# Selective scan in one core: a sequence's statistics in one slot, its normalising over three, one subtraction by halves

## The reference

```
xz = hidden_states @ in_proj_w.T
x, z = jnp.split(xz, 2, axis=-1)
...                                    # causal convolution of 4 taps, silu
delta = jax.nn.softplus(delta + dt_proj_b.reshape(N_HEADS, H_DIN))
def step(s, inp):
    d_t, u_t, B_t, C_t = inp
    dA = jnp.exp(d_t[..., None] * A)
    s = s * dA + (d_t * u_t)[..., None] * B_t[:, :, None, :]
    y_t = jnp.einsum('bhdn,bhn->bhd', s, C_t)
    return (s, y_t)
...
y = y + x * Dskip
y = y * jax.nn.silu(z)
```

## Time and profile before

| | us |
|---|---|
| median of three runs | 3590.76 |
| the profiled execution's own time | 3593.5 |
| its span, first to last instruction | 3591.7 |
| selective scan, first slots without a scan | 1880 to 1976.9 |
| selective scan, first to last scan step's end | 1976.9 to about 3014 |
| mixture and store after it | 3014 to 3591.7 |

### The profile page before, as it was taken

How to read it: one execution, slowest core, us unless ns; L and a number is a source line. 1 busy time by engine, 2 the same in 40 slices (tenths; PEclk the granted TensorE clock), 3 DMA queues, 4 the chain that set the end, 5 groups by cost and what they waited for, 6 DMA issues and landing times. The chain is left out here.

```text
span 3591.7 us, 45021 instructions
## 1 busy us (share of the span) xinstructions
PE 2679.7 (75%) x12336; PEld 1880.9 (52%) x12336; DVE 2211.8 (62%) x3886; ACT 1544.3 (43%) x2662; POOL 2124.8 (59%) x1697
## 2 busy tenths in 40 slices
PE   4699995997579998449983767867867866599900
PEld 4599982443468897429981322322322323389900
DVE  4766553675566564673320989989989887733312
ACT  4333334663433333423334556546646633433300
POOL 0477761322057776335544988988888685355467
PEclk9899996777589999559996889999999998599955
DMA  6011112000401111602232877878877876122222
GB/s 170 18 47 47 46 40 58 24 24 1 124 28 47 45 47 32 188 9 70 70 71 63 277 264 267 278 255 273 286 243 267 280 251 195 31 64 71 69 69 76
DMA packets 286348, 429.39 MB, mean 120 GB/s; under 512 B 58332, under 2 KB 195839, under 8 KB 286240
## 3 DMA queue, kind: packets, MB, share of 16 engines
q1 hardware_dynamic: 250784, 357.34, 30.2%
q0 software_dynamic: 35456, 70.86, 8.3%
HBM read 367.51 MB, written 62.39 MB: 120 GB/s over the span
## 5 line engine op out<-in xcount | busy, mean ns | idle before, releaser
L600 POOL DMA_INDIRECT m_rows<-rows_in,m_source x568 | 552.0, 972 | 361.8 <-PE m_T_ps L628 211.5
L1497 PE MATMUL s_y_ps<-s_prod,ident 128*128 128x512 f32 x1024 | 549.0, 664 | 281.1 <-DVE s_prod L1766 281.0
L1759 DVE TENSOR_TENSOR_SCAN s_dA<-s_dA,s_dBu 128x1024 f32<-128x1024 f32 x256 | 586.2, 2290 | 146.4 <-POOL s_dBu L1457 72.3
L1457 POOL TENSOR_TENSOR s_dBu<-s_du,s_B_row 128x1024 f32<-128x1024 f32 x256 | 602.8, 2358 | 104.5 <-DVE s_dA L1759 97.0
L634 PE MATMUL m_A_ps<-m_rowsT,m_own 128*128 128x256 f32 x2272 | 566.5, 382 | 2.0 <-ACT m_rowsT L681 1.1
L650 PE MATMUL m_Y_ps<-m_own,m_hid 128*128 128x128 f32 x4544 | 554.3, 275 | 3.6 <-issue 3.6
L650 PEld LDWEIGHTS m_Y_ps<-m_own,m_hid 128*128 128x128 f32 x4544 | 529.8, 192 | 5.7 <-issue 5.6
L1497 PEld LDWEIGHTS s_y_ps<-s_prod,ident 128*128 128x128 f32 x1024 | 192.0, 205 | 600.4 <-DVE s_prod L1766 404.7
L634 PEld LDWEIGHTS m_A_ps<-m_rowsT,m_own 128*128 128x128 f32 x2272 | 412.9, 192 | 48.3 <-ACT m_rowsT L681 1.9
L1587 ACT ACTIVATE s_dA<-s_delta,s_decay 128x1024 f32<-128x1024 f32 x256 | 285.6, 1118 | 336.3 <-DVE s_prod L1766 329.7
L691 ACT ACTIVATE m_act_a<-m_A_ps,m_own 128x256 f32<-128x256 f32 x568 | 238.5, 471 | 433.8 <-PE m_A_ps L634 302.5
(11 more groups left out here) (229 smaller groups left out, 3789.0 us busy)
## 6 DMA issues: line engine op xcount, KB each, us to landing
s_B_row<-s_bc_rows SPq DMA_DIRECT2D x256, 512.0 KB, 5.6
s_C_row<-s_bc_rows SPq DMA_DIRECT2D x256, 512.0 KB, 5.7
rows_out<-m_y_sb SPq DMA_DIRECT2D x142, 128.0 KB, 1.9
rows_in<-m_xs SPq DMA_DIRECT2D x64, 256.0 KB, 3.2
m_rows<-rows_in,m_source POOLq DMA_INDIRECT x568, 2.5
s_got<-rows_by_token SPq DMA_DIRECT2D x16, 512.0 KB, 5.1
m_got<-rows_by_token SPq DMA_DIRECT2D x32, 256.0 KB, 4.2
rows_by_token<-m_y_sb,m_target POOLq DMA_INDIRECT x284, 2.3
```

The lines of the kernel that those rows point to most:

```text
L600: pool.indirect_dma_start(rows[:, b % 2, r, :], None, c.rows_in, bass.IndirectOffsetOnAxis(source[:, 2 * b + r:2 * b + r + 1], 0)).then_in ...
L1457: nc.gpsimd.tensor_tensor(dBu[q % RING][:, :], du[s % 2][:, h, :], B_row[q % RING][:, :], ALU.mult).then_inc(dBu_ready, 1)
L1497: ins = nc.tensor.matmul(y_ps[:, at(cc, 512)], c.ident[:, :], prod[q % 2][:, at(cc, 512)], start=(n == 0), stop=(n == NS - 1))
L1759: nc.vector.tensor_tensor_scan(dA[q % 2][:, :], dA[q % 2][:, :], dBu[q % RING][:, :], 0.0, ALU.mult, ALU.add).then_inc(scanned, 1)
```

## The change

DVE: `scales(t)` moves from slot 6 to slot 5, right behind `statistics(t)`. POOL: `take_root(t)` moves from slot 7 to slot 6. ACT: the eight tiles of `normalise` are spread over slots 7 (four), 8 (two) and 9 (two). ACT: e1 - 1 becomes two operations over one half each, the first in slot 26 and the second in slot 27, behind the dA made in slot 27; POOL's subtraction of half h waits only for half h. The counts of the semaphore `soft_act` go from 6 to 7 in a sequence.

```diff
             def soften(t, h, i):
                 done = t * 4 * HALVES + 4 * h
                 if i == 0:
-                    pool.wait_ge(soft_act, t * 6 + 6)
+                    pool.wait_ge(soft_act, t * 7 + 6 + h)
...
-                if t is not None and i == 7:
+                if t is not None and i == 6:
                     take_root(t)
...
-            def normalise(t):
-                act.wait_ge(norm_step, t * 2 + 2)
-                if t > 0:
-                    Use("turned", t - 1, 1).read(act)
-                for j in range(TILES):
+            def normalise(t, tiles):
+                if 0 in tiles:
+                    act.wait_ge(norm_step, t * 2 + 2)
+                    if t > 0:
+                        Use("turned", t - 1, 1).read(act)
+                for j in tiles:
...
                 nc.scalar.activation(du[t % 2][:, :, :], e1[:, :, :], ACT.Ln).then_inc(soft_act, 1)
-                act.wait_ge(soft_act, t * 6 + 5)
                 for k in (2, 3):
                     Use("dt", t, k).taken(act)
-                nc.scalar.activation(e1[:, :, :], e1[:, :, :], ACT.Identity, bias=minus_one[:, :]).then_inc(soft_act, 1)
+
+            def rounded_part(t, h):
+                act.wait_ge(soft_act, t * 7 + 5)
+                nc.scalar.activation(e1[:, h, :], e1[:, h, :], ACT.Identity, bias=minus_one[:, :]).then_inc(soft_act, 1)
...
-                    if i == 9:
-                        normalise(t)
+                    if 7 <= i < 10:
+                        normalise(t, (range(4), range(4, 6), range(6, 8))[i - 7])
...
                     if i == 26:
                         logarithm(t)
+                    if 26 <= i < 28:
+                        rounded_part(t, i - 26)
...
                     if i == 5:
                         statistics(t)
-                    if i == 6:
                         scales(t)
```

More of the change, by code:

```diff
@@ L1658, in exponent @@
                 nc.scalar.activation(e[:, h, :], e[:, h, :], ACT.Exp, scale=-1.0).then_inc(soft_act, 1)
-                act.wait_ge(soft_act, t * 6 + h * 2 + 1)
+                act.wait_ge(soft_act, t * 7 + h * 2 + 1)
                 nc.scalar.activation(e1[:, h, :], e[:, h, :], ACT.Identity, bias=1.0).then_inc(soft_act, 1)
             def logarithm(t):
-                act.wait_ge(soft_act, t * 6 + 4)
+                act.wait_ge(soft_act, t * 7 + 4)
                 wait(act, dBu_ready, (t - 1) * ALLN)
                 nc.scalar.activation(du[t % 2][:, :, :], e1[:, :, :], ACT.Ln).then_inc(soft_act, 1)
-                act.wait_ge(soft_act, t * 6 + 5)
                 for k in (2, 3):
                     Use("dt", t, k).taken(act)
-                nc.scalar.activation(e1[:, :, :], e1[:, :, :], ACT.Identity, bias=minus_one[:, :]).then_inc(soft_act, 1)
+            def rounded_part(t, h):
+                act.wait_ge(soft_act, t * 7 + 5)
+                nc.scalar.activation(e1[:, h, :], e1[:, h, :], ACT.Identity, bias=minus_one[:, :]).then_inc(soft_act, 1)
             def step(q):
```

## The result

The changed kernel takes 3586.43 us (median of 12 runs, 3580.28 to 3590.37), the kernel before, run beside it, 3593.64 us (12 runs, 3589.01 to 3600.63). The ratio is 0.998, with a 95% interval of 0.9971 to 0.9989: 7.2 us faster, between 4.0 and 10.4.

A forecast was written before the change was run, and what follows sets the result against it. DVE sets the time, so only its waits count. Terms 6.2 + 2.2 + 0.2 - 0.2 + 1.6 = 10.0 us (unrounded 9.9) take 3590.8 to 3580.9 us; 8-in-10 range 3575 to 3587.5.

The forecast's parts named there:

- rival (c): Slot 28: the split gives nothing because POOL's chain or a row of B comes last there; 3587.1 us, chance 0.10.
- slot 28, seven windows: Half the subtraction leaves ACT's chain before scan 28, 0.88 us in each of seven windows, 6.2 us gained.
- slots 10 and 11, sequences 1 to 7: Fewer tiles ahead of ACT's z copies let scan 11 start earlier in sequences 2, 3 and 6; 2.2 us gained.
- slots 10 and 11, sequence 0: In sequence 0 about 0.2 us is free in slot 11.
- statistics, slots 5 and 6: Dependent aggregates lose 0.7 us, the small variance operation goes from 4.0 to 3.5 us over seven windows; 0.2 us lost together.
- first window: Before the first scan: the root starts 0.7 us earlier and the half subtraction saves 0.88; 1.6 us gained.
- 2.00 - 1.12 = 0.88: Slot 28: whole subtraction 2.00 us less a half taken as 1.12, so ACT's chain gets 0.88 us shorter.
- what is late next: After slot 28: POOL's chain moves by the same 0.88 us, so scan 32 isn't left behind; B_row could be.
- rival (e): POOL late in slot 6: a held gather costs from 2.1 us of hold on, 2.3 us once; seven times 3610.2, chance 0.02.
- one hold in 96 gathers speaks against it: The argument against a held gather in all seven windows: only one, of 5.54 us in sequence 5, was seen.
- The shared port: DVE's small variance operation waits for POOL's whole running product; in sequence 6 it goes from 1.29 to 2.15 us.

The follow-up runs named there:

- e_order: The changed kernel with the wait for Ln ahead of the two bank waits again, only the first half waiting; one run, 3740.39 us against 3753.92 before.
- e_split: The kernel before with only the subtraction halved; 3722.71 us against 3733.49 before, ratio 0.9971.
- e_move: The kernel before with all of the change but the halved subtraction; 3729.64 us, ratio 0.9991 to the kernel before.
- before_again: The kernel before, unchanged, run once more on another chip; one run, 3749.68 us.
- e_add7: The changed kernel with the second add_out in slot 7 instead of slot 9; 3710.69 us against 3753.92 before, ratio 0.9884.
- e_pool: The changed kernel with the two small operations on 8 columns made by POOL ahead of the root, instead of DVE; one run, 3740.33 us.
- e_root7: The changed kernel with the root back in slot 7 and the tiles in slots 8 (six) and 9 (two); one run, 3720.52 us.

## Why the prediction held, and where its sum was off

The sign and the size held, and the time lies inside the range: 3586.43, predicted 3580.9. Of the 5.5 us between them, 2.9 are the kernel before, whose 12 runs have a median of 3593.64 where the three had 3590.76. The other 2.7 are the gain: 7.2 us (4.0 to 10.4) where the sum said 9.9. The interval holds both figures, so the runs alone don't show that the sum was off, nor do they tell the forecast from rival (c), whose 3587.1 lies nearer; that takes the slots. There the two pairs of profiles put the stage's gain at 6.04 us where the terms for the stage add up to 8.4. The sum beside them:

| term | predicted | two profiles before to two after |
|---|---|---|
| slot 28, seven windows | -6.2 | -5.43 |
| slots 10 and 11, sequences 1 to 7 | -2.2 | -3.28 |
| slots 10 and 11, sequence 0 | -0.2 | -1.05 |
| statistics, slots 5 and 6 | +0.2 | +0.58 |
| slot 17 | none | +1.19 |
| held gather, sequence 5 slot 9 | none | +2.10 |
| first window | -1.6 | -2.5 |

Only slot 28 is the same in both pairs, and the statistics nearly so (0.45 and 0.71). The other rows are means of unlike values: slots 10 and 11 gained 3.9 and 2.7 us, in sequence 0 0.2 and 1.9, the hold cost 1.5 and 2.7, slot 17 1.0 and 1.4, the first window gained 1.7 and 3.4. It is luck, too, that slots 10 and 11 gave 1.9 us more than the sum had and so covered more than half of what slots 17 and 9 took.

**The split: right, mis-sized.** The term "2.00 - 1.12 = 0.88" measured 0.78. Half the subtraction takes 1.15 us and not 1.12, the nearest row I had taken (dA), and the rewritten order of waits costs 0.08, as e_order shows. Nothing came late behind it: rival (c) falls, with the step into slot 28 at 6.12 in all seven windows and slots 29 to 32 as before.

**The spread: right, a little small.** That ACT's tiles hold slot 11, and PE's z once they are gone, is shown by e_split against e_move. I counted 0.95 us at most for a window, with gains in three; the step into slot 11 gains 0.5 to 0.9 in sequences 1 to 5 and loses 0.3 in 6; in the second pair it gains 0.4 to 0.9 and loses 0.4. In sequence 7, which normalises nothing, it is 0.5 and 0.3 shorter as well. The working took the end of z in each sequence from the one trace of before as fixed, and it isn't: in before_again, the same kernel, it ends 2.20 us after scan 10 in sequence 1 and 2.52 in sequence 4, where the first trace had 3.75 and 3.65. In the changed kernel it is 2.90 or 2.91 in five of seven. That the granted clock decides this, by when PE is back at its upper level (2.4 GHz) in slot 9, fits the rows of PE in sequence 3, where the sum takes 3.07 us and the z behind it 1.89, but was not tried by itself. In the changed kernel the granted clock of 2398 to 2406 was 0.64, and PE was busy 3.32 us of those 8:

```profile
2398.00:2406.00 8.00, 3.32 (x5) 1.51 (x5) 4.76 (x4) 1.62 (x3) 7.64 (x5) 0.64 0.96 299
2412.00:2430.00 18.00, 18.00 (x44) 7.93 (x44) 17.83 (x11) 9.82 (x11) 16.23 (x10) 1.00 0.85 271
```

**Slot 17: a give-back that was missing.** The step that failed is the one on slot 11, "what is late next": I asked it of slot 28 and not here. The second row above shows PE busy 18.00 of 18 us in slots 12 to 16; before, the same slots (2415 to 2433) had 17.78. DVE's finish of the sum then waits 0.22 us for it, and the step into slot 17 is 4.84 instead of 4.50:

```profile
2431.02 1.28 DVE L1757 SCALAR_TENSOR_TENSOR s_y<-s_u,s_d_skip,s_y_ps 128x1024 f32<-128x1024 f32 x1 [0.22 <-PE s_y_ps L1497]
```

It is so in six windows after, in three (two in the second profile) before. e_split, without the spread, has 36.06 there, and every kernel with it 38.0 to 38.4, until e_add7 lets PE start its z earlier and has 36.24. That PE's backlog is the cause fits all of these rows; no run changed that backlog alone.

**The hold: a cost left out of the sum.** The prediction named the price in rival (e), from 2.1 us of hold on, 2.3 us once, and the row that showed a hold. Its price before was taken too high, 2.2 us by the length of the window; the step into slot 9 shows 1.37, and the rest of that window's excess lies in slots 11 and 17. What failed is the judgement "one hold in 96 gathers speaks against it". It does speak against seven holds, but the one that was in the trace belonged in the sum at its price, because nothing said that it would go away. It stood at the same gather in 13 of 14 profiles, and cost 2.10 us more on average than before. Of what the stage is short of its sum, 2.4 us, it is the largest piece; slot 17 comes next.

**The shared port: right.** The forecast for sequence 6 was 2.15 us, the trace has 2.16. In e_pool, where DVE has no such operation, the 2.16 us are gone. The Trainium skill, page "SBUF — State Buffer", section "Who interferes with whom", gives the port pair that VectorE and GpSimd share to whoever issues first, for the whole instruction. The row beside POOL's product agrees with it. The statistics cost 0.4 us more than the 0.2 predicted: over the seven windows the small operation got 0.3 us shorter (3.86 to 3.55, mean of two profiles) where 0.5 was predicted, and the rest of the move cost 0.9 where 0.7 was predicted.

**The first window** got 2.5 us shorter where 1.6 was predicted. The root starts 0.6 to 0.7 us earlier against the stage's start, as worked out. The rest can't be told: the kernel before takes 97.1 and 98.8 us for this window in its two profiles, and the kernels that have both the early root and the split take 93.5 (e_order) to 95.7 (e_pool).

## What to carry to other kernels

When an operation moves to an earlier slot, price the worst stall already seen on the queue it moves to: a stall with 4.2 us of cover before had 2.1 after, and the same hold cost 2 us more. When a wait is removed, ask what the released engine runs into some slots later, and not only in the next. And follow the longest wait that a change leaves standing back to its root before moving anything small: the shifted pieces brought 6 us of the stage, the one add that PE's bank was waiting for brought 31.

## What the runs showed of the hardware

- One gather, the 114th of 128 indirect transfers of the selective scan, was held at its issue for 3.8 to 5.5 us in 13 of 14 profiles, whatever the kernel did around it; no other was held over 0.31 us without a wait that explains it. Some profiles (before_again, e_add7, e_pool) name a matmul of PE's projection as what released it, others (before, after, e_split) nothing. With eight gathers more at the start it was not held and no other was in its place. What holds it stays open.
- Two satisfied waits ahead of the wait that decides cost 0.08 us on ACT (a gap of 0.11 us after, 0.03 in e_order), once in each window.
- Windows of different edits came out at the same 129.7 to 129.8 us (after, e_root7 and e_pool, sequences 2 to 4), though e_pool had won 0.4 us in slots 5 and 6: its last z ended 3.32 to 3.38 us after scan 10 where the other two have 2.90 or 2.91. It is no rule: e_order has 129.94, 129.19 and 130.08 there. What sets the end of z was read from the rows, and not tried by itself.
- The code outside the stage, untouched, moved by 3 us from one profile to the next, which is half of the gain under study. A change of this size is read in its own slots and not in the span.
